# Attention block on one core: softmax reciprocals spread through DRAM instead of through TensorE

## What is computed

```python
q = (x @ Wq.T).reshape(B, N, 12, 32)
k = (x @ Wk.T).reshape(B, N, 12, 32)
v = (x @ Wv.T + bv).reshape(B, N, 12, 32)
a = einsum('bnhd,bmhd->bhnm', q, k) * SCALE + adj[:, None]
a = where(all(a == 0, axis=-1), -inf, a)      # such rows end as 0
a = nan_to_num(softmax(a, axis=-1))
o = einsum('bhnm,bmhd->bnhd', a, v).reshape(B, N, 384)
out = layernorm(x + o @ Wo.T + bo)
```

## Time and profile before

| | |
|---|---|
| median of 3 runs | 718.36 us (717.56 to 718.78) |
| profiled execution | 718.51 us |
| its span, first to last instruction | 716.2 us |
| granted TensorE clock, mean | 0.997 |
| busy share PE, DVE, ACT, POOL | 98%, 84%, 86%, 68% |
| DMA moved | 184.61 MB, 258 GB/s mean |

### The profile page before, as it was taken

How to read it: one execution, slowest core, us unless ns; L and a number is a source line. 1 busy time by engine, 2 the same in 40 slices (tenths; PEclk the granted TensorE clock), 3 DMA queues, 4 the chain that set the end, 5 groups by cost and what they waited for, 6 DMA issues and landing times.

```text
span 716.2 us, 23143 instructions
## 1 busy us (share of the span) xinstructions
PE 698.7 (98%) x7557; PEld 600.7 (84%) x7557; DVE 600.1 (84%) x2220; ACT 613.8 (86%) x1993; POOL 487.2 (68%) x548
## 2 busy tenths in 40 slices
PE   8999999999999999999999999999999999999895
PEld 8878888888888888888888888888898888888774
DVE  4898988889888889888889888889888889888973
ACT  4889988889988889988888988889888888898882
POOL 4767666677766678766677766678766677766452
PEclk9999999999999999999999999999999999999998
DMA  8475877787777687777787777787777777777672
GB/s 266 152 278 206 300 267 264 252 315 236 263 263 273 241 309 240 265 264 267 251 302 240 262 267 259 252 305 247 257 270 261 262 291 248 255 273 259 248 288 90
DMA packets 84008, 184.61 MB, mean 258 GB/s; under 512 B 4272, under 2 KB 42928, under 8 KB 75696
## 3 DMA queue, kind: packets, MB, share of 16 engines
q1 hardware_dynamic: 83888, 183.12, 72.3%
HBM read 103.42 MB, written 79.69 MB: 256 GB/s over the span
## 4 chain that ended last, share of the span: by engine, by line
PE 85%; DVE 5%; DMA 4%; issue 2%; POOL 2%; ACT 1%; SPq 0%; DVEq 0%; ACTq 0%; POOLq 0%
PE bank_b L787 34%; PE bank_c L787 16%; PE bank_a L877 12%; PE s_bank L836 11%; PE bank_t L847 8%; PE bank_c L858 2%; DVE neg L1192 2%; DMA sq_dram<-w_f 2%; DMA sq_probT<-sq_dram 2%; ACT prob L559 1%; PE bank_t L858 1%; DVE w_f L1209 1%; DMA xt<-in_xT 1%; POOL kq_lo L400 0%; DVE y L1292 0%
## 5 line engine op out<-in xcount | busy, mean ns | idle before, releaser
L559 ACT ACTIVATE prob<-neg,negmax 128x256 f32<-128x256 f32 x768 | 380.3, 500 | 51.8 <-DVE w_f L1209 34.3
L1192 DVE CUSTOM_DVE_ANT_0 neg<-s_bank,bias_sq 128x256 f32<-128x256 f32 x512 | 185.2, 414 | 49.0 <-issue 42.6
L1209 DVE STREAM_TRANSPOSE w_f<-prob 128x512 f32<-128x512 f32 x256 | 173.2, 696 | 0.7 <-ACT prob L559 0.7
L559 ACT ACTIVATION_READ_ACCUMULATOR prob<-neg,negmax 128x1 f32 x768 | 147.7, 192 | 0.0
L400 POOL TENSOR_TENSOR kq_lo<-kq,kq_hi 128x512 fp32r<-128x512 f32 x96 | 125.2, 1304 | 7.7
L398 POOL CAST kq_hi<-kq 128x512 fp32r<-128x512 f32 x96 | 60.2, 627 | 79.3 <-issue 73.9
L787 PE MATMUL bank_c<-xt_hi,w_hi 128*128 128x256 f32 x384 | 111.1, 289 | 1.0 <-DVE w_lo L1171 1.0
L787 PE MATMUL bank_c<-xt_hi,w_lo 128*128 128x256 f32 x384 | 108.3, 282 | 0.0
L787 PE MATMUL bank_c<-xt_lo,w_hi 128*128 128x256 f32 x384 | 108.3, 282 | 0.0
L1192 DVE CUSTOM_DVE_ANT_0 neg<-s_bank,bias 128x256 f32<-128x256 f32 x256 | 91.0, 420 | 15.2 <-PE s_bank L836 15.0
L847 PE MATMUL bank_t<-ident,prob 128*128 128x128 f32 x512 | 80.3, 279 | 0.7 <-ACT probT L569 0.7
(11 more groups left out here) (88 smaller groups left out, 1794.1 us busy)
## 6 DMA issues: line engine op xcount, KB each, us to landing
sq_dram<-w_f SPq DMA_DIRECT2D x64, 1024.0 KB, 4.5
sq_probT<-sq_dram SPq DMA_DIRECT2D x64, 1024.0 KB, 5.6
xt<-in_xT SPq DMA_DIRECT2D x32, 384.0 KB, 4.5
xr<-in_x SPq DMA_DIRECT2D x32, 384.0 KB, 6.2
out_y<-y_out SPq DMA_DIRECT2D x31, 384.0 KB, 3.0
bias<-in_adj SPq DMA_DIRECT2D x32, 256.0 KB, 3.2
w_f<-in_wkT SPq DMA_DIRECT2D x3, 192.0 KB, 4.5
w_f<-in_wqT SPq DMA_DIRECT2D x3, 192.0 KB, 5.0
```

What stands on the lines that cost most here:

```text
L559: nc.scalar.activation(prob[:, u % PROB_RING, k], neg[:, h, w.c], ACT.Exp, scale=-1.0, bias=negmax[t.p][:, w.c, h:h + 1], accum_out=sums[t ...
L1192: nc.vector.tensor_tensor_reduce(out=neg[:, h, w.c], in0=s_bank[h % JH][:, w.c, :], in1=by[t.p][:, w.c, :], scale=-1.0, scalar=BIG, op0=AL ...
L1209: nc.vector.transpose(sq_stage[w.g][:, :, a:a + PAIR, :, w.c].rearrange("p b h m s -> p (h m) b s"), prob[:, u % PROB_RING].rearrange("p k ...
```

## The change

Reciprocals: `widen_inv`, `spread` and `save_o` go. VectorE inverts the sums, which lie in another order, into a tile of 32 columns (24 used), turns that tile in 32x32 blocks (`turn_inv`), SP stores it to DRAM (16 KB, pieces of 128 B) and loads it back as `inv_all` (each of the four heads' rows to 32 partitions, 3 KB a partition, 384 KB). VectorE divides straight out of the weighed bank in three pieces of 256 columns, so that a `weigh` now waits for the division of the group before. V1's bias: ScalarE copies V1 out of the bank, GpSimd adds the bias in SBUF. `flag` writes into bank_t. `o_n` has two buffers.

```diff
+            def store_inv(t):
+                sp.wait_ge(inv_turned, t.count(1, 1))
...
+                sp.dma_start(inv_dram[t.p].rearrange("k b r -> b k r"),
+                             inv_t[:]).then_inc(inv_stored[t.p], DMA)
+            def load_inv(t):
+                sp.wait_ge(inv_stored[t.p], t.loads())
...
+                sp.dma_start(inv_all[t.p][:].rearrange("p g n -> p (g n)"),
+                             inv_dram[t.p][0:JH * KC * NT].rearrange("(j k) b r -> j (k b r)", j=JH).unsqueeze(1)
+                             .to_broadcast([JH, HD, KC * N])).then_inc(inv_loaded[t.p], DMA)
...
-                nc.gpsimd.tensor_copy(inv_wide[:], inv[:].unsqueeze(3).to_broadcast([P, NT, H, HD])
-                                      ).then_inc(inv_wide_ready, 1)
+            def add_bv(t):
+                pool.wait_ge(b_loaded, 2 * DMA)
+                pool.wait_ge(v_copied, t.count(1, 1))
...
+                nc.gpsimd.tensor_tensor(v[t.p][:, 1, :], v[t.p][:, 1, :], bv_all[:], ALU.add).then_inc(v_saved[1], 1)
...
-            def save_o(t, g):
+            def copy_v(t):
...
+                nc.scalar.activation(v[t.p][:, 1, :], bank_at(t, "V1")[:, 0:D], ACT.Copy).then_inc(v_copied, 1)
...
+                nc.vector.reciprocal(inv[:, 0:H * NT], sums[t.p][:].rearrange("p j g c -> p (j g c)")
+                                     ).then_inc(inv_ready, 1)
+            def turn_inv(t):
+                dve.wait_ge(inv_ready, t.count(1, 1))
...
+                nc.vector.transpose(inv_t[:], inv[:]).then_inc(inv_turned, 1)
+            def divide(t, g):
+                dve.wait_ge(pv_done[g], t.count(1, 1))
+                if g == 0:
+                    dve.wait_ge(inv_loaded[t.p], t.loads())
...
+                nc.vector.tensor_tensor(o_n[t.p][:, g, :], bank_at(t, f"PV{g}")[:, 0:N], inv_all[t.p][:, g, :],
                                         ALU.mult).then_inc(o_n_ready, 1)
```

More of the change, by code:

```diff
@@ L336, in end @@
                 t31 = Batch(31)
+                store_squares(t29, 1)
+                load_squares(t29, 0)
+                store_out(t26)
+                store_inv(t29)
+                load_bias(t31)
+                load_squares(t29, 1)
+                load_xr(t29)
+                load_inv(t29)
+                store_squares(t30, 0)
                 store_squares(t30, 1)
+                store_out(t27)
                 load_squares(t30, 0)
+                store_inv(t30)
                 load_squares(t30, 1)
+                load_inv(t30)
                 store_squares(t31, 0)
@@ L344, in end @@
                 store_out(t28)
+                store_inv(t31)
                 load_squares(t31, 1)
+                load_inv(t31)
+                load_xr(t31)
                 store_out(t29)
-                load_xr(t31)
                 store_out(t30)
@@ L351, in _ @@
             start()
-            for c in range(3, 30):
+            for c in range(3, 29):
                 step(Batch(c))
@@ new lines, in start @@
+                pe.wait_ge(kq_saved["Q12"], t2.count(1, 1))
+                project_kq(t3, "K01")
+                copied(t0, 11)
+                flag(t1)
+                pe.wait_ge(o_n_ready, t0.count(KC, 1))
+                weigh(t0, 1)
+                scores(t2, 0)
+                pe.wait_ge(flag_read, t1.count(1, 1))
+                transposes(t1, 8)
+                pe.wait_ge(o_n_ready, t0.count(KC, 2))
+                weigh(t0, 2)
+                pe.wait_ge(kq_saved["K2Q0"], t3.count(1, 1))
@@ L981, in start @@
-                project_kq(t3, "Q12")
+                pe.wait_ge(kq_saved["K01"], t3.count(1, 1))
+                project_kq(t3, "Q12")
+                scores(t2, 2)
+                pe.wait_ge(o_n_ready, t0.count(KC, 3))
+                weigh(t1, 0)
+                pe.wait_ge(v_copied, t2.count(1, 1))
+                project_y(t0, 0)
+                pe.wait_ge(kq_saved["Q12"], t3.count(1, 1))
+                project_kq(t4, "K01")
+                copied(t1, 11)
+                flag(t2)
@@ L1069, in end @@
                 t31 = Batch(31)
+                scores(t29, 2)
+                copied(t28, 10)
+                transposes(t28, 11)
+                pe.wait_ge(kq_saved["K2Q0"], t30.count(1, 1))
+                project_v(t29, 1)
+                pe.wait_ge(kq_saved["K01"], t30.count(1, 1))
+                project_kq(t30, "Q12")
+                pe.wait_ge(o_n_ready, t28.count(KC, 1))
+                weigh(t28, 1)
+                pe.wait_ge(v_copied, t29.count(1, 1))
+                project_y(t27, 0)
```

775 lines of the change are left out of this document (411 added, 364 removed).

## The result

The changed kernel takes **842.37 us** (median of 4 runs, 833.85 to 844.02) where the kernel before takes 718.49: a ratio of 1.1696 (95% interval 1.1625 to 1.1767). Forecast were 704.4 and 698 to 716. The profiled execution took 833.85 us, its span 832.1; it was the fastest of the four.

The account below looks back on a forecast made before the run. TensorE, without gaps, was taken as the bound: span 716.2 less 11.9 (29 batches at 0.41), 1 for the tail and 1 for filling is 702.3; with 2.3 around the span, less 0.15, 704.4 us, range 698 to 716.

Parts of the forecast that it names:

- the 21.04: TensorE's step in us: 21.45 less 0.41, from 0.65 for six transposes removed less 0.24 for dearer shape changes.
- the sum's better end: TensorE's step if the new order's changes of tile shape cost nothing: 0.65 us less a step.
- the flag's change of shape: On TensorE, the flag's matmul directly behind weighing pays 0.105 us for the changed tile shape.
- VectorE: Load of 19.7 us a step, net -0.2, including 1.55 for reading the flag and branching; slack 1.3 against 21.04.
- ScalarE: Loses three copies (0.81 us) and gains one of 384 columns (0.4): 18.5 us a step, slack 2.5.
- Rival B: VectorE becomes the bound through waits of 1.6 us a step: step 21.3, 7 us less gain, 711; chance 0.21.
- The store: The 16 KB of reciprocals to DRAM in pieces of 128 B: 2.2 us latency, bounded by 1.9 and 4.5.
- rival C: Late reciprocals hold TensorE once store plus load exceed 9.8 us; at 11 us 737, at 13.5 us 804; chance 0.12.
- The formula: A DMA costs about 2.0 us plus bytes over 436 GB/s: store 2.04, load 2.9; the forecast used the rows instead.
- The load: The 384 KB of reciprocals back to SBUF, likened to the xt load's 4.5 us: 5 us, behind the load of squares.
- Behind it stand load_squares(t,1), wanted only at 6.9 of the next step, load_xr and load_xt: On SP, store_inv waits until 16.7 of the step; load_inv lands at 2.9 of the next; no new wait ends last.
- The DMA share: Share of the DMA engines, 0.76 before, rises to 0.84 with 0.41 MB more a step.

Follow-up runs that it names:

- e3: Changed kernel without store and load of the reciprocals and without SyncE's wait for turn_inv, division by a constant (another output): 698.76 us, 0.9728.
- e13: e1 with load_xt moved behind load_squares(t,0) and load_xr behind store_squares(nxt,0) in SyncE's list: 717.85 us, 1.0002.
- e7: e1 with load_squares(t,1) ahead of store_inv and load_inv, and load_xt moved up behind load_squares(t,0): 804.59 us, 1.1197.
- e8: e1 with the loop's store and load of the reciprocals issued by ScalarE, between its exponentials, and not by SyncE: 878.71 us, 1.2172.
- e1: Changed kernel with the reciprocals' load as four DMAs, one per head, so that all 16 engines take part: 747.36 us, 1.0411.
- e4: Changed kernel, store and load kept on four engines, but nobody waits for the load and division takes a constant (another output): 841.94 us, 1.1722.
- e6: e4 with the load of e1, four DMAs over all engines: 746.6 us, 1.0409.
- e14: Changed kernel with the two order edits of e13 alone, the load still one DMA on four engines: 774.1 us, 1.0788.
- e15: e13 with GpSimd's xt_lo waiting for VectorE's zero_max in the steady steps: 714.58 us, 0.9943.
- e11: Kernel before the change plus an unused load of 256 KB a step on four engines: 718.76 us, 1.0012.

## Why the prediction was wrong

**TensorE and the engines beside it** were forecast well. The step without the transfers is 20.85 us, under the 21.04 and near the sum's better end (20.80). One term can be pointed at, in TensorE's timeline of e3:

```profile
401.69 0.19 PE L937 MATMUL bank_t<-zero_max,ones 128*128 128x24 bf16 x1
401.80 0.39 PE L900 MATMUL s_bank<-kq_hi 32*128 32x256 f32 x4
402.02 0.29 PE L900 MATMUL s_bank<-kq_lo,kq_hi 32*128 32x256 f32 x4
402.14 0.29 PE L900 MATMUL s_bank<-kq_hi,kq_lo 32*128 32x256 f32 x4
```

The flag behind weighing takes 0.11 and the first scores 0.22, 0.10 over their sisters. For the flag's change of shape alone I had 0.105: that is nearly all of the 0.11, so at most little is charged there. The other 0.1 us I haven't placed. VectorE was forecast at 19.7 with 1.55 of flag reading, so 18.15 busy; it is 17.76. ScalarE: 18.5, it is 18.65. Rival B did not come. Without the transfers the steady gain is 27 x (21.45 - 20.85) = 16 us, and e3 has 18.6 in all beside its own runs of before; its 698.76 is 5.6 under the forecast.

**The store** was sized well where its queue is nearly free: 1.9 us in most steps of e13, 1.9 to 5.1 in after with a median near 3, forecast 2.2. Its pieces of 128 B took 13 ns each, twice as long for a byte as the load's 3 KB pieces (178 ns), but 32 of them on each of four engines are 0.4 us in all. The Trainium skill, *DMA: Bandwidth & Descriptors*, section Specifications, which rival C named, says that pieces under 512 B are done as read-modify-write. It gives no price there. The 3 us more that the rival needed would have to lie in these 0.4, and they do not. Where the store did take 3 us more (e7, e8) it stood behind other transfers. The formula that the forecast takes from the Trainium skill, *DMA: Bandwidth & Descriptors*, section Anatomy of one DMA, is given there for DMAs issued from GpSimd, while SyncE issues these. Its 2.9 us for the load is a third of what after shows.

**The load** is the term of the sum that failed: forecast 5, measured 8.2 to 11.1 in after (median 9.7), and 6.8 on sixteen engines in e1, 6.2 in e13, so that it was sized too small even there. I compared it by bytes with the xt load and did not ask how many engines its pattern uses.

**"Behind it stand load_squares(t,1), wanted only at 6.9 of the next step, load_xr and load_xt"** (behind store_inv) is the step of the argument that failed with it, and by e4 the dearer one: with the load in the queue and nobody waiting for it, the time is the same. I asked who waits for the DMAs behind store_inv, and not what the landings of the squares' stores, which the list waits for twice a step, become with 0.4 MB more in the queue. They were taken as unchanged (4.5) and are 8.8 in after, 7.8 in e1. By that SyncE's list itself becomes the longest ring: 27 us in the step shown, 25.2 for a step on the mean. I had counted load_inv as issued when the 16 KB land; it was held until load_squares(t,1) had gone, 1.7 us more.

**The DMA share** was forecast at 0.84 and is 0.83 in e13, at 20.85 to 21.63 us a step. A share under one says nothing on latency: in the stretch of after shown above it is 0.78, with stores of squares landing after 9.8 and 12.0 us.

**Rival C** had the sign, a place where TensorE stops, and the size of store and load together: some 12.8 us by the medians of after, within its 9.8 to 13.5. Its reason does not stand in this list: by e4 and e6 cutting the ring from the division back to the division changes nothing. By its own rule 12.8 us would have given 704.4 + 27 x 3.0 = 785, against 842 measured. In the list of e14, where VectorE waits 70.0 us ahead of its divisions, the experiment of e4 was not made, and there the ring may bind.

**Shown and open.** The loss comes with the transfers (e3); both the four engines (e1, and e4 against e6) and the order of the list (e13) make it, and what each is worth depends on which is mended first. The 19 us between e13 and e3 are settled in part: e15 gives 3.3 back; of its 17.6 us of span over e3, 7 lie between the fifth and the twenty-eighth weighing of group 0, where the divisions wait for late loads in some steps, 6 ahead of that and 5 behind it. What makes some of these loads later than others stays open. What part of the 124 us is the lower clock was not measured either; as an estimate, work done in the 88 us at 1.2 GHz would take half as long at 2.4, so that the clock's own part is 44 us at most.

## What to carry to other kernels

Before a DMA is costed by its bytes, look at the slowest dimension of both its patterns: at 4 the load here ran on four engines, at 32 on sixteen, and the four also held the last parts of the DMAs behind it. Then follow the issuing engine's list as a ring of its own: sum the landings that it waits for within a step, at the lengths that they will have with the new bytes in the queue, and compare that with the step; a small transfer with a chain behind it goes ahead of large ones. And test the wait that the profile shows last by cutting it alone, since it may only be where another ring's delay surfaces.

## What the runs showed of the hardware

- A load of 384 KB whose slowest dimension is 4 landed in four parts after 8.2 to 11.1 us (median 9.7); as four DMAs over sixteen engines it took 6.8 from first issue to last landing (e1). In the step shown of after, four parts of each DMA issued behind it landed 2.5 to 4 us behind the other twelve. In a list with room 256 KB on four engines cost nothing (e11, 1.0012).
- A 16 KB store landed in 1.9 to 2.6 us in the steady steps of e13, where it is issued ahead of a 1 MB load, and in 4.7 to 5.9 in e7, where it is issued behind it; issued from another engine's queue it did not pass the transfers under way (5.4 to 8.7, e8).
- A VectorE instruction of 24 columns took 1.64 us in place of 0.18 when it began 0.22 us behind a subtraction of GpSimd, and ended with it.
- With TensorE idle for 14% of the span the granted clock was 0.947; in e3, where it has no pauses in the steady step, 0.997. In after TensorE idled 3.95 us ahead of its weighing at 446.94; from 448 to 454 us the granted clock was 0.59, so mostly the 1.2 GHz level, and the scores' matmuls started 0.21 us apart, where they started 0.12 apart at 437, at 2.4 GHz.
